# Kernel with four attention layers: reloads of the first layer's split weights issued at another place of ScalarE's program

## The chip, the cores and the metric

The kernel runs on one core of a Trainium2 chip. The metric is the device time of one execution in microseconds (us); lower is better. The core has TensorE (matmuls; PE in the profile, its weight loads PEld), VectorE (DVE), ScalarE (ACT), GpSimd (POOL) and SyncE (SP), and 16 DMA engines that serve the transfers issued by any of them.

## The reference, cut to what matters

Four layers follow each other. Only the first is touched. It is attention over 16 heads of 64 channels, for 8 batch elements of 512 positions, with two sets of weights, one for each half of the positions:

```python
for i in range(2):                                   # columns 0:256 and 256:512
    h = jnp.einsum('od,bdl->bol', Wq_list[i], z1ss[:, :, s:e])
    h = h + jnp.einsum('od,bdl->bol', Wi_list[i], u1ss[:, :, s:e])
q, k, v = jnp.split(w_heads, 3, axis=1)
rq = q + r_w_bias[None, :, :, None]
score = jnp.einsum('bndi,bndj->bnij', rq, k) * SCALE
prob = jax.nn.softmax(score, axis=-1)
attn_vec = jnp.einsum('bnij,bndj->bndi', prob, v)
attn_out = jnp.einsum('od,bdl->bol', Wo, attn_vec) + bo[None, :, None]
x = attn_out + z1ss                                  # then a layer norm
```

Here z1ss and u1ss have 8 x 256 x 512 elements and all is float32. The other three layers (a recurrent one, two attentions with an MLP, a non-local block) follow unchanged.

## The kernel before

`l0_attention` splits its work into 64 units (`HALF`). A unit is one batch element and one pair of heads; unit n has `bp, pair, l = where(n)`: turn `bp` (4 turns of two batch elements), `pair` of heads (8) and lane `l` (which of the turn's two elements). So two neighbouring units use the same weights, and each pair of heads comes back in every turn.

For precision each operand is held as a high and a low part, and a product is three matmuls. The weights of queries and keys for a pair are `w_hi[i]` and `w_lo[i]` with i = pair % 2: two buffers of 1 MB for each part. The value weights cover two pairs and lie in one buffer for each part, `wv_hi` and `wv_lo`. In the first turn (units 0 to 15) they are split on the chip and stored to DRAM (`w_scratch`, `wv_scratch`). In the three later turns they are only loaded back: `load_w`, L683 to L692, on ScalarE's DMA queue. With t = pair counted over all turns (8 to 31), there are 24 loads for each part of w, and 12 for each part of wv (even t alone). A load into w[i] must come after the last projection that used pair t-2, and ahead of the first that uses pair t.

Each engine runs a program written out by hand over n; semaphores alone tie them. TensorE in iteration n does: first half of the scores of unit n (L453), the projections of queries and keys for unit n+1 (L419, 48 matmuls), second half of the scores, the sums' transposes of n-1 (L462), the output projection of n-2 (L492), the weighing of values of n-1 (`weigh_values`, L478, 32 matmuls in two halves f = 0 and f = 1), and, if pair(n+1) is even, the value projection of unit n+1 (L437, 48 matmuls). So of four iterations two have a value projection: n = 3 and 0 (mod 4) do, 1 and 2 don't. Matmuls for w of pair t start in iteration 2t-1 (unit 2t).

ScalarE in iteration n: exponentials of the first half (L576), `queries(n+1)` (L599), `outputs(n-2)`, `keys(n+1)` (L583), `sums(n-1)`, exponentials of the second half, then `load_w`, then first-turn splits, `weighed(n-1)`, `values(n+1)`. `load_w` is called with part = 1-l: in iteration 2t-3 (l = 1) the high part of pair t, with `wv_hi` ahead of it if t is even, and in iteration 2t-2 (l = 0) the low part, with `wv_lo` ahead of it if t is even. Ahead of them stands a wait for the projections that used the buffer (`projected`).

The probabilities of a unit are turned in two halves: VectorE transposes 32x32 blocks in place (L778), then 16 DMAs of 64 KB for each half move the blocks from `prob` to `probT` (L281, `move`): 9 on SP's queue and 7 on POOL's. POOL does its part behind `scale_outputs` and `spread_sums`. Half f = 0 of unit n is moved in the middle of iteration n, half f = 1 at the start of iteration n+1; both are used by `weigh_values(n)` late in iteration n+1. A ring of three buffers (`RING`) makes ScalarE's exponentials wait for the half moved three halves before (`half_moved`).

SyncE also issues loads of x and u and of the accumulators, and their stores, at the start of a turn (`load_x`, `load_acc`, `store_acc`).

Of the kernel before, what the change touches and what calls it, by code (L numbers as in the profile page):

```python
# [6 lines left out]
F32 = mybir.dt.float32  # L7
# [11 lines left out]
LANES = 2  # L19
TURNS = B // LANES  # L20
# [134 lines left out]
def l0_attention(nc, kept, first, d, x, u, att, x1):  # L155

    D, HP = 64, 8
# [7 lines left out]
    QUADS = HP // 2  # L165
# [7 lines left out]
    def where(n):  # L173

        t, l = n // LANES, n % LANES
        return t // HP, t % HP, l
# [19 lines left out]
    def scratch(name, shape):  # L196
        return nc.dram_tensor(name, shape, F32, kind="Internal").ap()

    w_scratch = [scratch(f"kept_w_{part}", (HP, P, KT, 2, 2, P)) for part in ("hi", "lo")]
    wv_scratch = [scratch(f"kept_wv_{part}", (QUADS, P, KT, 2, 2, P)) for part in ("hi", "lo")]  # L200

    with Phase(nc, "l0") as ph:
# [4 lines left out]
        w_hi, w_lo = [[ph.sb(f"w_{part}{i}", [P, KT, 2, 2, P], F32R) for i in range(2)] for part in ("hi", "lo")]  # L207
        wv_hi, wv_lo = [ph.sb(f"wv_{part}", [P, KT, 2, 2, P], F32R) for part in ("hi", "lo")]
# [23 lines left out]
        w_stored, wv_stored = [ph.sem(f"w_stored{i}") for i in range(2)], ph.sem("wv_stored")  # L232
        w_in, wv_in = [ph.sem(f"w_in{i}") for i in range(2)], ph.sem("wv_in")
# [23 lines left out]
        def full(eng, s):  # L257

            eng.wait_ge(s.full, s.k + 1)
# [5 lines left out]
        def half_moved(eng, i):  # L265

            eng.wait_ge(moved_sp[i % RING], 16 * BY_SP * (i // RING + 1))
            eng.wait_ge(moved_pool[i % RING], 16 * (len(MOVES) - BY_SP) * (i // RING + 1))
# [15 lines left out]
        def projected(eng, n):  # L284

            full(eng, S[f"v{n}_1"] if where(n)[1] % 2 == 0 else S[f"k{n}"])

        with ph.block() as block:
# [278 lines left out]
            def _(act):  # L567
                def exponentials(n, its):
                    i = 2 * n + its[0] // 2
                    if i >= RING:  # L570
                        half_moved(act, i - RING)
                    for it in its:
                        for h in H2:
                            s = S[f"s{n}_{it}{h}"]
                            act.wait_ge(max_ready, 2 * IT * n + 2 * it + h + 1)
                            act.activation(prob[i % RING][:, :, it % 2, h, :].rearrange("p (q t) s -> p t q s", q=Q),  # L576
                                           s.ap[:, :].rearrange("p (t q s) -> p t q s", t=IT, q=Q), ACT.Exp, bias=nmax[:, n % 2, it, h:h + 1],
                                           accum_out=rsum[:, n % 2, it, h:h + 1]).then_inc(s.drained, 1)

                def keys(n):  # L580
                    s, l = S[f"k{n}"], where(n)[2]
                    full(act, s)
                    act.activation(k_hi[l][:, :], s.ap[:, :], ACT.Copy, scale=SCALE).then_inc(k_hi_ready, 1)  # L583
# [11 lines left out]
                def queries(n):  # L595
                    bp, pair, l = where(n)
                    s = S[f"q{n}"]
                    full(act, s)
                    act.activation(q_hi[l][:, :], s.ap[:, :], ACT.Identity, bias=rb[:, pair:pair + 1]).then_inc(q_hi_ready, 1)  # L599

                def sums(n):
                    s = S[f"r{n}"]
                    full(act, s)
                    act.wait_ge(scaled, n)
                    act.activation(rT[:, :], s.ap[:, :], ACT.Copy).then_inc(s.drained, 1)
# [8 lines left out]
                def outputs(n):  # L614
                    act.wait_ge(scaled, n + 1)
                    if n:
                        full(act, S[f"w{n - 1}_{RT - 1}"])
                    act.activation(oT_hi[:, :], oT[:, :], ACT.Copy).then_inc(oT_hi_ready, 1)
# [7 lines left out]
                def split_w(p):  # L626
                    act.wait_ge(wraw_in, 16 * p)
                    if p >= 2:
                        projected(act, LANES * (p - 2) + 1)
                        act.wait_ge(w_stored[p % 2], 32 * (p // 2))  # L630
                    act.activation(w_hi[p % 2][:, :, :, :, :], wraw[:, :, :, :, :], ACT.Copy).then_inc(w_hi_ready, 1)
# [8 lines left out]
                def split_wo():  # L640
                    act.wait_ge(wo_in, 16)
                    act.activation(wo_hi[:, :, :], wo_raw, ACT.Copy).then_inc(wo_hi_ready, 1)
# [39 lines left out]
                    for r in range(RT):  # L682
                        act.activation(xf[:, r, :], xf[:, r, :], ACT.Identity, bias=nb[:, r:r + 1], scale=sd[:, r:r + 1]).then_inc(xn_ready, 1)  # L683

                def load_w(t, part):
                    p, i = t % HP, t % 2
                    projected(act, LANES * (t - 2) + 1)
                    if i == 0:
                        act.wait_ge(wv_stored, 32 * QUADS)
                        act.dma_start((wv_hi, wv_lo)[part][:, :, :, :, :].bitcast(F32), wv_scratch[part][p // 2]).then_inc(wv_in, 16)  # L690
                    act.wait_ge(w_stored[i], 32 * QUADS)
                    act.dma_start((w_hi, w_lo)[part][i][:, :, :, :, :].bitcast(F32), w_scratch[part][p]).then_inc(w_in[i], 16)  # L692

                for h in H2:
                    own = slice(h * RT, (h + 1) * RT)
# [12 lines left out]
                for n in range(HALF):  # L708
                    bp, pair, l = where(n)
                    exponentials(n, (0, 1))  # L710
                    if n + 1 < HALF:
                        queries(n + 1)
                    if n > 1:
                        outputs(n - 2)
                    if n + 1 < HALF:
                        keys(n + 1)
                    if n:
                        sums(n - 1)
                    exponentials(n, (2, 3))
                    t = (n - 1) // LANES + 2  # L720
                    if HP <= t < TURNS * HP:
                        load_w(t, 1 - l)
                    if n == 0:
                        split_wo()
                    if bp == 0 and l == 0 and pair + 1 < HP:
                        split_w(pair + 1)
                    if bp == 0 and l == 1 and pair % 2 == 0 and pair + 2 < HP:
                        split_wv(pair // 2 + 1)
                    if pair == HP - 1 and bp + 1 < TURNS:
                        split_x(bp + 1, l)  # L730
                    if n == BIAS:
                        bias_rows()
                    if n == CENTRE:
                        centred()
                    if n:
                        weighed(n - 1)
                    if n + 1 < HALF:
                        values(n + 1)
                    if n == SUMMED:
                        moments()  # L740
                    if n == NORMED:
                        normed()
# [2488 lines left out]
```

## Time and profile before

| what | value |
|---|---|
| median of 3 runs | 3445.14 us (3443.86 to 3448.17) |
| the profiled execution's own time | 3442.56 us |
| its span, first to last instruction | 3440.5 us |
| granted TensorE clock, mean over the span | 0.949 |
| TensorE busy | 3115.6 us, 91% of the span |
| first layer | the first 1,300 us of the span, about 38% |

The durations below come from the one profiled execution. Its own time is 2.1 us over its span and 2.6 us under the median of the runs. A granted clock of 1.00 in a stretch is TensorE's full clock of 2.4 GHz, 0.5 is 1.2 GHz.

### The profile page before, as it was taken

The page shows a single profiled execution, that of the slowest core. Times are in us where ns is not written, and L with a number is a line of the kernel's source. Part 1 is how long each engine was busy: PE and PEld are TensorE (multiplying, and loading weights), DVE is VectorE, ACT ScalarE, POOL GpSimd, SP SyncE. Part 2 cuts the span into 40 slices and gives each one's busy share as a digit, 9 for nine tenths or more (in the row PEclk, how much of TensorE's full clock was granted, in tenths as well). Part 3 has the DMA queues.
Part 4 walks back from the last instruction along what each step waited for, and adds up shares of the span by engine and source line. Part 5 has one row for each costly group of instructions (what it writes and reads, how often), then busy time and mean ns, then how long its engine had stood idle before and what let it go on. Part 6 is the DMA issues. An engine that isn't in the chain of part 4 may idle for free. (4 is left out here: it accounts for less than half of the span.)

```text
span 3440.5 us, 55581 instructions
## 1 busy us (share of the span) xinstructions
PE 3115.6 (91%) x20384; PEld 2400.2 (70%) x20384; DVE 2362.2 (69%) x3589; ACT 1742.2 (51%) x4185; POOL 701.2 (20%) x1207
## 2 busy tenths in 40 slices
PE   7998999999998996799999997589999999699998
PEld 6777777777777774566666664378887787488885
DVE  6776666666675662999999999257777888543212
ACT  4454444544454543355566553247777777432222
POOL 2444444544444441000000000011101111000000
PEclk9999999999999998899999998789999999899999
DMA  7668766666675655445555444210011110310004
GB/s 245 209 218 268 225 184 183 207 212 197 197 234 162 207 143 187 121 96 123 116 117 120 104 109 104 59 64 14 26 56 56 44 44 29 108 50 12 25 13 167
DMA packets 179676, 434.78 MB, mean 126 GB/s; under 512 B 52912, under 2 KB 61104, under 8 KB 154960
## 3 DMA queue, kind: packets, MB, share of 16 engines
q1 hardware_dynamic: 120256, 262.17, 26.9%
q10 hardware_dynamic: 28304, 106.09, 8.6%
q0 software_dynamic: 30848, 62.97, 7.3%
q8 instruction: 164, 2.69, 0.3%
q14 instruction: 104, 0.85, 0.1%
HBM read 233.95 MB, written 62.91 MB: 86 GB/s over the span
## 5 line engine op out<-in xcount | busy, mean ns | idle before, releaser
L281 POOL DMA_DIRECT2D l_probT<-l_prob x896 | 441.2, 500 | 258.6 <-DVE l_prob L778 238.8
L756 DVE TENSOR_REDUCE l_nmax<-l_bank 128x1 f32<-128x512 f32 x512 | 317.0, 681 | 198.2 <-PE l_bank L453 198.2
L576 ACT ACTIVATE l_prob<-l_bank,l_nmax 128x512 f32<-128x512 f32 x512 | 344.5, 688 | 135.1 <-DVE l_nmax L756 120.5
L419 PE MATMUL l_bank<-l_x_hi,l_w_hi 128*128 128x256 f32 x1024 | 307.6, 300 | 75.4 <-DMA l_w_lo<-kept_w_lo 54.5
L778 DVE STREAM_TRANSPOSE l_prob<-l_prob 128x1024 f32<-128x1024 f32 x256 | 314.4, 1228 | 16.3 <-DVE l_acc L799 9.7
L419 PE MATMUL l_bank<-l_x_hi,l_w_lo 128*128 128x256 f32 x1024 | 299.8, 293 | 0.0
L419 PE MATMUL l_bank<-l_x_lo,l_w_hi 128*128 128x256 f32 x1024 | 299.0, 292 | 0.0
L1817 DVE TENSOR_TENSOR_SCAN l_kv<-l_wx,l_kv 128x2056 f32<-128x2056 f32 x64 | 283.8, 4435 | 3.1 <-DVE l_sxc L1938 1.5
L419 PEld LDWEIGHTS l_bank<-l_x_hi,l_w_hi 128*128 128x128 f32 x1024 | 207.0, 202 | 99.5 <-DMA l_w_lo<-kept_w_lo 59.2
L2391 ACT ACTIVATE l2a_sc<-l2a_sc,l2a_nmax 128x256 f32<-128x256 f32 x512 | 254.7, 508 | 41.1 <-DVE l2a_nmax L2507 41.1
L478 PE MATMUL l_bank<-l_probT,l_v 128*64 128x256 f32 x2048 | 248.6, 397 | 25.9 <-issue 12.5
L478 PEld LDWEIGHTS l_bank<-l_probT,l_v 128*64 128x64 f32 x2048 | 147.9, 142 | 121.6 <-issue 44.0
L2507 DVE CUSTOM_DVE_ANT_0 l2a_sc<-l2a_sc,l2a_mb 128x256 f32<-128x256 f32 x512 | 217.1, 484 | 0.0
L419 PEld LDWEIGHTS l_bank<-l_x_hi,l_w_lo 128*128 128x128 f32 x1024 | 207.1, 202 | 0.0
L419 PEld LDWEIGHTS l_bank<-l_x_lo,l_w_hi 128*128 128x128 f32 x1024 | 206.7, 202 | 0.0
L2500 DVE SCALAR_TENSOR_TENSOR l2a_sc<-l2a_bank,l2a_m 128x512 f32<-128x512 f32 x256 | 158.7, 681 | 54.1 <-PE l2a_bank L2263 54.1
L380 POOL TENSOR_TENSOR l_oT<-l_oT,l_rT 128x512 f32<-128x512 f32 x64 | 99.8, 1559 | 455.5 <-ACT l_oT L612 455.5
L2871 DVE TENSOR_TENSOR l2b_h_lo<-l2b_hf,l2b_h_hi 128x512 fp32r<-128x512 f32 x64 | 44.0, 691 | 199.3 <-ACT l2b_h_hi L2814 199.3
L2807 ACT ACTIVATE l2b_hf<-l2b_bank,l2b_b 128x512 f32<-128x512 f32 x64 | 44.0, 688 | 255.4 <-PE l2b_bank L2749 255.4
L1809 DVE TENSOR_TENSOR l_kv<-l_vb,l_ik 128x2048 f32<-128x2048 f32 x64 | 145.9, 2279 | 6.4 <-DMA l_vb<-vd 5.9
L437 PE MATMUL l_bank<-l_wv_hi,l_x_hi 128*128 128x256 f32 x512 | 148.1, 289 | 1.9 <-DVE l_wv_lo L815 1.9
L2274 PE MATMUL l2a_bank<-l2a_ident,l2a_sc 128*128 128x128 f32 x1024 | 133.2, 277 | 16.6 <-DVE l2a_oT L2520 8.7
(348 smaller groups left out, 7989.3 us busy)
## 6 DMA issues: line engine op xcount, KB each, us to landing
l_probT<-l_prob SPq DMA_DIRECT2D x1152, 64.0 KB, 2.7
l_vb<-vd SPq DMA_DIRECT2D x64, 1024.0 KB
l_probT<-l_prob POOLq DMA_DIRECT2D x896, 64.0 KB, 2.4
l_w_hi<-kept_w_hi ACTq DMA_DIRECT2D x24, 1024.0 KB, 7.2
l_w_lo<-kept_w_lo ACTq DMA_DIRECT2D x24, 1024.0 KB, 7.7
l_wv_hi<-kept_wv_hi ACTq DMA_DIRECT2D x12, 1024.0 KB, 5.4
l_wv_lo<-kept_wv_lo ACTq DMA_DIRECT2D x12, 1024.0 KB, 5.6
kept_w_hi<-l_w_hi SPq DMA_DIRECT2D x8, 1024.0 KB, 9.8
```

Source lines behind the costliest of these rows:

```text
L281: eng.dma_start(probT[i % RING][r * SQ:(r + 1) * SQ, g, :, :, :, :], prob[i % RING][g * SQ:(g + 1) * SQ, r * IT:(r + 1) * IT, :, :, :]).th ...
L419: mm = pe.matmul(s.ap[:, c * ROWS:(c + 1) * ROWS], a[:, kt, c, g, :], b[:, kt, c * ROWS:(c + 1) * ROWS], start=m == 0, stop=m == 3 * KT - 1)
L437: mm = pe.matmul(s.ap[:, at], a[:, kt, jt * P:(jt + 1) * P], b[:, kt, c, :, :], start=m == 0, stop=m == 3 * KT - 1)
L478: mm = pe.matmul(s.ap[own, f * ROWS:(f + 1) * ROWS], v[l][:, pair % 2, j, own], half[:, :, :, j, h, :], start=j == 0, stop=j == IT - 1)
L576: act.activation(prob[i % RING][:, :, it % 2, h, :].rearrange("p (q t) s -> p t q s", q=Q), s.ap[:, :].rearrange("p (t q s) -> p t q s", t ...
L756: dve.tensor_reduce(nmax[:, n % 2, it, h:h + 1], s.ap[:, :], AX.X, ALU.max, negate=True).then_inc(max_ready, 1)
L778: dve.transpose(own, own).then_inc(turned, 1)
L1809: dve.tensor_tensor(kv[n % NK][:, :, 1:ROWS + 1], vb[n % NV][:, :, :], ik[:, ct, :].unsqueeze(1).to_broadcast([P, NJ, ROWS]), ALU.mult).th ...
L1817: dve.tensor_tensor_scan(own, wx[:, :, :].rearrange("p j t -> p (j t)"), own, 0.0, ALU.mult, ALU.add)\
L2391: ins = act.activation(to[:, r, :], to[:, r, :], ACT.Exp, scale=-1.0, bias=nmax[:, k % SC_RING, i, r:r + 1], accum_out=rsum[:, k % SC_RING ...
L2500: dve.scalar_tensor_tensor(out=sc[k % SC_RING][i][:, :, :], in0=s.ap[:, :].rearrange("p (r j) -> p r j", r=RT), scalar=HD ** -0.5, in1=own ...
L2507: dve.tensor_tensor_reduce(out=to[:, r, :], in0=to[:, r, :], in1=own[:, r, :], scale=-1.0, scalar=3.0e38, op0=ALU.add, op1=ALU.min, accum_ ...
```

## The change

In turns 1 to 3 the loads are issued elsewhere in ScalarE's program. Both parts of w for pair t go out in one iteration, 2t-3, right behind the first half's exponentials and ahead of `queries(n+1)`. The two parts of wv go out in the next iteration, 2t-2, at the same place, for even t. The number of loads, their sizes, their queue and the semaphores they count on are unchanged.

```diff
-                def load_w(t, part):
+                def load_w(t):
                     p, i = t % HP, t % 2
                     projected(act, LANES * (t - 2) + 1)
-                    if i == 0:
-                        act.wait_ge(wv_stored, 32 * QUADS)
-                        act.dma_start((wv_hi, wv_lo)[part][:, :, :, :, :].bitcast(F32), wv_scratch[part][p // 2]).then_inc(wv_in, 16)
                     act.wait_ge(w_stored[i], 32 * QUADS)
-                    act.dma_start((w_hi, w_lo)[part][i][:, :, :, :, :].bitcast(F32), w_scratch[part][p]).then_inc(w_in[i], 16)
+                    for part, to in enumerate((w_hi, w_lo)):
+                        act.dma_start(to[i][:, :, :, :, :].bitcast(F32), w_scratch[part][p]).then_inc(w_in[i], 16)
+
+                def load_wv(g):
+                    projected(act, LANES * 2 * (g - 1) + 1)
+                    act.wait_ge(wv_stored, 32 * QUADS)
+                    for part, to in enumerate((wv_hi, wv_lo)):
+                        act.dma_start(to[:, :, :, :, :].bitcast(F32), wv_scratch[part][g % QUADS]).then_inc(wv_in, 16)
...
                     exponentials(n, (0, 1))
+                    t = (n - 1) // LANES + 2
+                    if HP <= t < TURNS * HP:
+                        if l == 1:
+                            load_w(t)
+                        elif t % 2 == 0:
+                            load_wv(t // 2)
                     if n + 1 < HALF:
                         queries(n + 1)
...
                     exponentials(n, (2, 3))
-                    t = (n - 1) // LANES + 2
-                    if HP <= t < TURNS * HP:
-                        load_w(t, 1 - l)
```

## Rows read from the trace of the kernel before

**Rows 1.** The page: busy time of each engine.
```profile
PE 3115.6 (91%) x20384; PEld 2400.2 (70%) x20384; DVE 2362.2 (69%) x3589; ACT 1742.2 (51%) x4185; POOL 701.2 (20%) x1207
```

**Rows 2.** Waits of PE, 311 to 1290 us: total, times, longest.
```profile
PE l_bank L419 <- DMA l_w_lo<-kept_w_lo: 54.5, 11, 6.8
...
PE l_bank L478 <- DMA l_probT<-l_prob: 1.2, 1, 1.2
```

**Rows 3.** Busy time by stretch: iterations 20 to 23, one each.
```profile
core 0: us, PE busy (x) PEld busy (x) DVE busy (x) ACT busy (x) POOL busy (x), PEclk, DMA share, GB/s
433.93:454.59 20.66, 20.66 (x163) 17.38 (x162) 12.93 (x18) 9.65 (x23) 8.67 (x17) 1.00 0.51 155
454.59:469.30 14.71, 14.71 (x115) 11.56 (x114) 12.44 (x18) 8.46 (x21) 3.53 (x8) 1.00 0.46 137
469.30:484.02 14.72, 14.72 (x116) 11.64 (x114) 12.93 (x19) 8.46 (x21) 8.67 (x16) 1.00 0.93 278
484.02:512.39 28.37, 22.74 (x164) 19.46 (x162) 13.52 (x19) 9.66 (x23) 13.80 (x25) 0.88 0.67 190
```

**Rows 4.** Timeline of PE, end of iteration 22 and start of 23.
```profile
480.42 3.67 PE L478 MATMUL l_bank<-l_probT,l_v 128*64 128x256 f32 x32
484.02 0.50 PE L453 MATMUL l_bank<-l_k_hi,l_q_hi 64*128 64x512 f32 x2
...
491.33 0.58 PE L419 MATMUL l_bank<-l_x_hi,l_w_hi 128*128 128x256 f32 x1 [5.63 <-DMA l_w_lo<-kept_w_lo]
```

**Rows 5.** Timeline of ACT in iteration 22: exponentials, q_hi, the last issue.
```profile
471.10 0.69 ACT L576 ACTIVATE l_prob<-l_bank,l_nmax 128x512 f32<-128x512 f32 x1 [1.08 <-DVE l_nmax L756]
...
474.08 0.69 ACT L599 ACTIVATE l_q_hi<-l_bank,l_rb 128x512 fp32r<-128x512 f32 x1 [0.20 <-PE l_bank L419]
...
479.62 0.68 ACT L576 ACTIVATE l_prob<-l_bank,l_nmax 128x512 f32<-128x512 f32 x1
...
481.13 0.45 ACTq L692 DMA_DIRECT2D l_w_lo<-kept_w_lo  x1
```

**Rows 6.** The low part of w issued at 481.1: issue to landing.
```profile
DMA to landing us min/median/max: 10.2/10.2/10.2
```

**Rows 7.** All 48 loads of w (L692): issue to landing.
```profile
DMA to landing us min/median/max: 4.8/7.3/11.4
```

**Rows 8.** Busy time by stretch: iterations 15, 19, ..., 47 and 59 (ten).
```profile
327.08:355.13 28.05, 22.92 (x166) 19.59 (x164) 18.59 (x23) 11.39 (x24) 13.21 (x20) 0.88 0.65 197
...
1199.19:1228.79 29.60, 23.04 (x164) 19.75 (x163) 13.53 (x19) 9.65 (x23) 13.80 (x25) 0.88 0.64 183
sum 281.01, PE 227.18 PEld 194.24 DVE 152.79 ACT 102.08 POOL 138.86; mean PE 22.72 PEld 19.42 DVE 15.28 ACT 10.21 POOL 13.89
```

**Rows 9.** Moves on SP's queue, 469.6 to 475.8 us (durations, first and last start).
```profile
L281 SPq DMA_DIRECT2D l_probT<-l_prob x9: 507/597/912, 469.8 to 475.7; - x9
...
DMA to landing us min/median/max: 3.7/3.9/6.1
```

**Rows 10.** Moves on POOL's queue in the same stretch, from its timeline.
```profile
471.88 3.47 POOL L281 DMA_DIRECT2D l_probT<-l_prob  x7
```

**Rows 11.** Moves on SP's queue, 448.9 to 454.6 us.
```profile
L281 SPq DMA_DIRECT2D l_probT<-l_prob x9: 507/592/894, 449.1 to 454.5; - x9
...
DMA to landing us min/median/max: 2.0/2.8/3.1
```

**Rows 12.** DMA queues, 468 to 472 us: packets, MB, share; issues below.
```profile
q10 hardware_dynamic: 212, 1.61, 95.9%
...
l_probT<-l_prob SPq DMA_DIRECT2D x4, 64.0 KB, 4.1
```

**Rows 13.** DMA queues, 476 to 480 us (q0 is POOL's, q1 SP's).
```profile
q0 software_dynamic: 261, 0.55, 59.3%
q1 hardware_dynamic: 272, 0.37, 38.9%
```

**Rows 14.** Timeline of PE in iteration 14, second half of weigh_values.
```profile
325.20 0.44 PE L478 MATMUL l_bank<-l_probT,l_v 128*64 128x256 f32 x2 [1.18 <-DMA l_probT<-l_prob]
```

## The prediction

> **What bounds the kernel now.** I read four views in this order. The page first: TensorE is busy 91% of the span, every other engine less [rows 1]. An average over four layers proves little, so next the busy time by stretch, cut at the starts of four iterations of the first layer, in the steady state of turn 1 [rows 3]. The reader is to see that in iterations 20, 21 and 22 TensorE is busy for the whole stretch at a granted clock of 1.00 (2.4 GHz): 20.66 us with a value projection, 14.7 without. VectorE, the next one, has 12.9 of 14.7 us. Iteration 23 does the same work as iteration 20 and takes 28.37 us, at a clock of 0.88. Third, the waits of TensorE alone: one line holds 54.5 us in 11 waits, on the load of the low part of w [rows 2]. Fourth, the timeline there: the first half's scores start at 484.02, and the first projection starts at 491.33 after 5.63 us of nothing [rows 4]. That load was issued at 481.13 and took 10.2 us: 481.1 + 10.2 = 491.3, the very start of the matmul [rows 5, 6]. So in this place the end is set by when ScalarE issues a load, and everywhere around it by TensorE.
>
> The waits come at even t alone. There the low part of w is issued right behind `wv_lo`, and in an iteration without a value projection, so it has 14.7 us less what ScalarE has used up: from 481.13 to the wish of TensorE at 485.7 is 4.6 us, for a load that takes 4.8 to 11.4 [rows 4, 5, 7].
>
> **What the removed waits are worth.** Ten iterations (n = 15, 19, 23, ..., 47 and 59) have this wait. Together they last 281.01 us [rows 8]. Without it each would last what iteration 20 lasts, so 281.01 - 10 x 20.66 = 74.4 us. That is more than the waits themselves (54.5 with the eleventh, of 0.7 in iteration 51, whose stretch is long for other reasons; 53.8 for the ten). The rest, 20.6 us or 2.1 each, is TensorE at its lower level of 1.2 GHz: the clock fell during the wait and rose again some matmuls after it, and the stretch has 22.74 us of busy TensorE where iteration 20 has 20.66 [rows 3]. It goes with the waits: the undisturbed stretches around show 1.00.
>
> **The change part by part.** *Loads of w.* Pair t's two parts are now issued in iteration 2t-3, behind the first half's exponentials. In iteration 22 these start at 471.10, 1.8 us into the iteration; the issue stood 1.5 us behind the first exponential of its half (479.62 to 481.13), so now it comes about 3.0 to 3.3 us into an iteration [rows 3, 5]. TensorE wants w 1.7 us into iteration 2t-1 [rows 4]. For even t that is two iterations of 14.7 less 1.5: 28 us; for odd t two of 20.66: 40 us. The slowest of all loads took 11.4 us [rows 7]. The wait is gone with over 15 us to spare.
>
> *Loads of wv.* They are issued 3 us into iteration 2t-2 and wanted at the end of iteration 2t-1, behind `weigh_values`: 11.7 + 14.7 = 26 us. Also early enough.
>
> *ScalarE's program.* The number of issues is the same, 72. Two now stand ahead of `queries(n+1)`; they take 0.33 to 0.45 us each of the sequencer, some 0.8 together [rows 5]. Four exponentials of 0.69 us are then still to run, to 473.9, and q_hi can't start before 474.08, when TensorE has the product [rows 5]. So I cost this at nothing. If that cover were gone it would be 0.8 x 36 = 29 us on ScalarE, which is busy 8.5 of 14.7 us, so still not on the path. The wait `projected` ahead of the loads asks for the projection of unit 2t-3, which TensorE did in iteration 2t-4, ahead of any score of iteration 2t-3: it holds back neither the loads nor `queries`, `keys` and the second exponentials that are queued behind it. The stores it also waits for are those of the first turn; the last were issued one to three iterations earlier.
>
> *What is late next: the moves of the probabilities.* This is the unknown term. The loads share the 16 DMA engines with 64 moves of 64 KB in two iterations. In iteration 22 SP issues the nine moves of the second half of unit 21 from 469.8 to 475.7 and the last lands 6.1 us later, at 481.8; POOL issues its seven from 471.88 [rows 9, 10]. `weigh_values` starts at 480.42 and needs that half after half of its 3.67 us, at 482.25 [rows 4]. So 0.4 us are left today, with two loads issued 3.4 to 3.8 us ahead of the moves. The quiet case is at 449.1: last issue 454.5, landed 3.1 later, 8.5 us in all [rows 11]. Put at 469.8 it would end at 478.3, 3.9 us ahead of the need.
>
> After the change the two loads go out at about 472.3, 2.5 us behind the first move, not 3.4 ahead. From 468 to 472 the loads' queue had 95.9% of all 16 engines and moved 1.61 MB, 0.42 MB a us, while four moves already issued stood still [rows 12]; two loads of 1.05 MB so hold the engines for 5.0 us. Lower bound of the lateness: 0, if the moves get turns between (a gain is excluded, since TensorE has nothing else to win there). Middle: all 5.0 us fall on the moves, 478.3 + 5.0 = 483.3, 1.05 us late. Upper: a load takes 10.2 us [rows 6], landing at 482.8, and the half of the moves left over then drains at the rate that moves alone reach, 0.92 MB in 4 us, so 0.5 MB in 2.2 [rows 13]: 485.0, 2.8 us late.
>
> How often: moves of a second half stand in this window in iterations that follow one without a value projection, n = 2 and 3 (mod 4). In the other two they are issued before the iteration begins (449.1 against 454.59) and are done when the loads go out. Loads fall there for wv (12 times, n = 2) and for odd t of w (12 times, n = 3): 24 places. I take 0.5 us each, between nothing and 1.05, because before a load starts about 40% of the moves are through and a queue with little left needs few turns: 24 x 0.5 = 12 us. Ends: 0 and 24 x 2.8 = 67. A wait of this kind exists already, 1.2 us once [rows 2, 14], and shows what it looks like.
>
> **Sum.** Against the profiled execution's own time: 3442.6 - 74.4 - 0.7 + 12 = 3379.5. The median of the runs is 2.6 above that execution: 3382 us.
>
> **The rivals.** (1) *The moves aren't hurt at all.* The loads only rearrange 16 engines' work that fits: a share of 0.93 in iteration 22, 0.46 in iteration 21 [rows 3]. Then 3370 us. For it: the queues take turns of some sort, since moves did land by 481.8. Against it: the loads held 95.9% of the engines while moves waited [rows 12]. The Trainium skill, "DMA: Bandwidth & Descriptors", section "Queues, rings and completion order", has it that each engine takes turns among the queues, a packet of typically 9 to 17 descriptors at a time. By that rule the moves would lose little, and the result would be this rival's 3370; the trace agrees only in part [rows 11, 12], since the moves issued there landed 4.1 us after issue, against 2.8 in the quiet case.
>
> (2) *The moves starve*: 2 to 2.8 us late at 24 places, 48 to 67 us, gives back most of the gain: 3418 to 3437, say 3425. For it: 0.4 us are left now, and the DMA share is 0.93 already. Against: before, the loads delayed them too, from 8.5 to 12.0 us, and TensorE didn't wait.
>
> (3) *The other side: TensorE waits at `weigh_values` for over 3.1 us at 24 places.* From there 24 x 3.1 = 75 us eat the gain. With waits of 4 us the clock falls too (2.1 each): 24 x 6.1 = 146, so 3370 + 146 = 3516. It needs moves landing 16 us after the first issue where they have taken 12.0.
>
> (4) *The change does nothing*, since something else ends the wait at the same moment (x split, VectorE): 3445. Against: iteration 20 does all that iteration 23 does, in 20.66 us.
>
> **How the numbers follow.** My forecast (some lateness, 3374 to 3400) gets 0.52, rival 1 0.19, rival 2 0.18, rival 3 0.04, rival 4 0.03; 0.04 lies between them. The range goes from 3366 (rival 1 less the scatter of the runs) to 3416, which leaves out most of rival 2 and rivals 3 and 4. What a measurement of this kernel can tell from no change is 0.2%, 6.9 us: faster means below 3438. Faster 0.91, same 0.05, slower 0.04.
>
> **What would show it.** In the profile after: no wait of L419 on a load of w, iterations 15, 19, 23 and so on at 20.7 us and clock 1.00; a mean clock above 0.949; a line "PE L478 <- DMA l_probT" in the waits, with some 12 us in up to 24 waits. If that line has 40 or more, rival 2 holds; if it is still near 1.2, rival 1. The prediction is wrong if iterations n = 2 and 3 (mod 4) grow by 3 us or more, or if the long iterations stay at 26 to 30 us.

## The result, and the profile after

The changed kernel takes 3486.66 us (median of 4 runs, 3486.11 to 3489.57), the kernel before 3444.5 (4 runs, 3443.21 to 3448.17). The ratio is 1.0122 with a 95% interval of 1.0105 to 1.014: 42 us slower, where I had forecast 63 us faster. The profiled execution took 3489.57 us.

The page of the changed kernel, its span and the busy time of each engine:

```profile
span 3487.6 us, 55569 instructions
...
PE 3125.5 (90%) x20384; PEld 2394.4 (69%) x20384; DVE 2361.4 (68%) x3589; ACT 1743.5 (50%) x4185; POOL 699.7 (20%) x1207
```

Every engine has the same work as before [rows 1]. What changed is who waits. The waits of TensorE from 311 to 1338 us, to be read against [rows 2]:

```profile
PE l_bank L478 <- DMA l_probT<-l_prob: 61.9, 19, 8.0
PE l_bank L478 <- issue: 19.8, 2, 10.6
PE l_bank L492 <- ACT first_anx L659: 7.8, 1, 7.8
```

The wait of L419 on a load of w is gone, all 54.5 us of it. In its place stands a wait of L478, `weigh_values`, on the moves of the probabilities, which had 1.2 us. The busy time by stretch of the changed kernel, iterations 20 to 24, against [rows 3]:

```profile
core 0: us, PE busy (x) PEld busy (x) DVE busy (x) ACT busy (x) POOL busy (x), PEclk, DMA share, GB/s
447.38:468.04 20.66, 20.66 (x164) 17.37 (x163) 12.93 (x18) 9.67 (x23) 8.66 (x17) 1.00 0.36 98
468.04:482.75 14.71, 14.71 (x115) 11.55 (x115) 12.44 (x18) 8.47 (x21) 3.52 (x8) 1.00 0.76 242
482.75:504.78 22.03, 16.68 (x117) 12.21 (x116) 13.40 (x19) 8.47 (x21) 8.67 (x16) 0.85 0.72 193
504.78:527.76 22.98, 20.99 (x164) 17.41 (x162) 12.92 (x18) 9.67 (x23) 13.81 (x25) 0.99 0.77 214
527.76:548.42 20.66, 20.66 (x163) 17.37 (x162) 13.02 (x18) 9.56 (x23) 8.69 (x17) 1.00 0.37 105
```

Iteration 23 fell from 28.37 to 22.98 us, but iteration 22, which took 14.72, takes 22.03: the pair went from 43.09 to 45.01. The timeline of TensorE in the changed kernel, in iteration 22, and then the one wait in iteration 23, shows where:

```profile
493.87 1.95 PE L478 MATMUL l_bank<-l_probT,l_v 128*64 128x256 f32 x16
...
501.16 0.69 PE L478 MATMUL l_bank<-l_probT,l_v 128*64 128x256 f32 x2 [5.35 <-DMA l_probT<-l_prob]
...
519.95 0.44 PE L478 MATMUL l_bank<-l_probT,l_v 128*64 128x256 f32 x2 [1.99 <-DMA l_probT<-l_prob]
```

The first half of `weigh_values` runs on time; the second is ready at 495.81 (501.16 less 5.35) and its probabilities are not there until 501.1. The wait of 5.35 us and 1.97 us of lower clock (16.68 busy us, where the quiet iteration has 14.71) are the 7.31 us by which the iteration grew. TensorE's granted clock went from 2.4 to 1.2 GHz at 498.26, within the wait, and back at 505.09, just inside iteration 23.

The sum by iteration, 0 to 62, comes to 45.7 us, of 47.1 by which the span grew:

| iterations | before | after | difference |
|---|---|---|---|
| the ten long ones (15, 19, ..., 47, 59) | 281.0 | 260.5 | -20.5 |
| n = 2 (mod 4), from 14 to 58 | | | +52.5 |
| 0, 4, 16, 48, 51, 55 | | | +13.8 |
| n = 0 and 1 (mod 4) in the steady state | 20.66, 14.71 | 20.66, 14.71 | 0 |

The ten would last 206.6 us without any wait. So of the 74.4 us to be had, 53.9 were given back in the very same iterations, 25.8 of them in iterations 19 and 35 (33.19 and 33.91 us), at the starts of turns. In the third row, iterations 16 and 48 (2.4 and 3.5 us longer) have waits of L419, and the inputs are late there: SP's loads of x and u for the next turn landed 4.6 to 6.9 us after their issue before, 12.0 to 15.2 after, and ScalarE, which has to split them, now waits (311 to 1338 us):

```profile
ACT l_x_hi L624 <- DMA l_xraw<-in_u: 22.6, 3, 8.2
```

Now from the late half back to its cause. ScalarE's queue in the changed kernel, iteration 22: the last two loads, and `q_hi` behind them:

```profile
486.31 0.33 ACTq L696 DMA_DIRECT2D l_wv_hi<-kept_wv_hi  x1
...
486.67 0.46 ACTq L696 DMA_DIRECT2D l_wv_lo<-kept_wv_lo  x1
...
487.52 0.69 ACT L599 ACTIVATE l_q_hi<-l_bank,l_rb 128x512 fp32r<-128x512 f32 x1 [0.19 <-PE l_bank L419]
```

Then SP's moves of the wanted half (483.2 to 488.9 us), with the time from issue to landing, to be read against [rows 9, 11]:

```profile
L281 SPq DMA_DIRECT2D l_probT<-l_prob x9: 507/594/997, 483.3 to 488.8; - x9
...
DMA to landing us min/median/max: 1.9/4.9/12.3
```

The moves were issued on time: nine in 5.5 us (5.9 before). The last landed 12.3 us after its issue, at 501.1; the quiet case has 3.1 [rows 11], the case with loads ahead 6.1 [rows 9]. The issues are not late; the transfers are slow. The DMA queues of the changed kernel from 489 to 496 us (packets, MB, share of 16 engines; q10 holds the loads, q0 POOL's moves, q1 SP's):

```profile
DMA packets 510, 2.25 MB, mean 321 GB/s; under 512 B 124, under 2 KB 124, under 8 KB 299
...
q10 hardware_dynamic: 227, 1.73, 78.1%
q0 software_dynamic: 144, 0.32, 15.1%
q1 hardware_dynamic: 139, 0.20, 9.9%
```

In 7 us the moves' two queues got 0.52 MB, the wanted half and the unit's own first half together. In the 5 us after it, as the loads ended, they got 1.06 MB:

```profile
q1 hardware_dynamic: 442, 0.60, 55.1%
q0 software_dynamic: 234, 0.46, 40.8%
q10 hardware_dynamic: 25, 0.07, 6.2%
```

From here on I use one measure: L, from the first issue of a half's 16 moves to the last landing, for the half that `weigh_values` needs. The medians are over units 21 to 46: those whose half is used in iterations n = 2 (mod 4), seven of them, and those used in n = 3, six of them without unit 34 at the start of a turn. TensorE needs the half 12.55 us after the first issue in n = 2 (483.26 to 495.81 in iteration 22) and some 13 after it in n = 3. Before, L had a median of 9.9 us in n = 2 and 10.4 in n = 3; after, 16.2 and 15.7.

### The profile page after: what moved, and what is told of

It is laid out like the page before. It is cut to its first block and busy times, and to the rows that moved or that the text cites. A ratio compares the mean times of both kernels' runs of the same rounds, so it can differ in the third digit from the quotient of the medians.

```text
span 3487.6 us, 55569 instructions
## 1 busy us (share of the span) xinstructions
PE 3125.5 (90%) x20384; PEld 2394.4 (69%) x20384; DVE 2361.4 (68%) x3589; ACT 1743.5 (50%) x4185; POOL 699.7 (20%) x1207
## 3 DMA queue, kind: packets, MB, share of 16 engines
q1 hardware_dynamic: 120256, 262.17, 26.8%
## 5 line engine op out<-in xcount | busy, mean ns | idle before, releaser
L478 PE MATMUL l_bank<-l_probT,l_v 128*64 128x256 f32 x2048 | 266.6, 414 | 109.4 <-DMA l_probT<-l_prob 66.6
L419 PE MATMUL l_bank<-l_x_hi,l_w_hi 128*128 128x256 f32 x1024 | 298.1, 291 | 24.9 <-DVE l_x_lo L854 11.3
L478 PEld LDWEIGHTS l_bank<-l_probT,l_v 128*64 128x64 f32 x2048 | 152.0, 147 | 214.3 <-DMA l_probT<-l_prob 76.1
L419 PE MATMUL l_bank<-l_x_hi,l_w_lo 128*128 128x256 f32 x1024 | 291.3, 284 | 0.0
L419 PE MATMUL l_bank<-l_x_lo,l_w_hi 128*128 128x256 f32 x1024 | 291.1, 284 | 0.0
L419 PEld LDWEIGHTS l_bank<-l_x_hi,l_w_hi 128*128 128x128 f32 x1024 | 197.7, 193 | 48.6 <-issue 39.4
L419 PEld LDWEIGHTS l_bank<-l_x_hi,l_w_lo 128*128 128x128 f32 x1024 | 198.0, 193 | 0.0
L419 PEld LDWEIGHTS l_bank<-l_x_lo,l_w_hi 128*128 128x128 f32 x1024 | 197.9, 193 | 0.0
```

Source lines behind the costliest of these rows:

```text
L419: mm = pe.matmul(s.ap[:, c * ROWS:(c + 1) * ROWS], a[:, kt, c, g, :], b[:, kt, c * ROWS:(c + 1) * ROWS], start=m == 0, stop=m == 3 * KT - 1)
L478: mm = pe.matmul(s.ap[own, f * ROWS:(f + 1) * ROWS], v[l][:, pair % 2, j, own], half[:, :, :, j, h, :], start=j == 0, stop=j == IT - 1)
```

## The experiments

**Place or grouping (four runs).** Theory A: what costs is the place of the issue, about 3 us behind the first of the moves; the new grouping by itself is good. Rival: the grouping costs, 2 MB at once. The first run keeps the grouping and goes back to the old place:

```diff
                     exponentials(n, (0, 1))
-                    t = (n - 1) // LANES + 2
-                    ...
-                            load_wv(t // 2)
...
                     exponentials(n, (2, 3))
+                    t = (n - 1) // LANES + 2
+                    ...
+                            load_wv(t // 2)
```

> The new grouping (both parts of w in iteration 2t-3, both of wv in 2t-2), but issued at the old place, behind the second half's exponentials. Theory A (the loss comes from the place: loads that go out 3 us behind the first move stand amid the moves of the half that weigh_values needs next): 3370 to 3385 us, the waits of L478 on moves near 0 to 10 us, the moves of iteration 22 landed about 10 to 12 us after the first issue. Rival B (4 MB of moves and loads in one short iteration are too much for the DMA engines, wherever in it the loads go out; the grouping does it): 3440 to 3490 us, waits of L478 on moves over 40 us.

Measured: 3382.45 us (3373.22 to 3395.5), ratio 0.9815 (0.9778 to 0.9851), mean clock 0.956. The busy time by stretch of this run, iterations 22 and 23:

```profile
455.95:470.66 14.71, 14.71 (x116) 11.56 (x114) 12.92 (x19) 8.47 (x21) 8.70 (x16) 1.00 0.88 275
470.66:491.32 20.66, 20.66 (x164) 17.37 (x162) 13.42 (x19) 9.67 (x23) 13.85 (x25) 1.00 1.02 303
```

Both iterations are at their floor, the second with the DMA engines full throughout. L is 10.3 and 11.0 us, under 12.55. A gain of the forecast size is in the grouping, at the old place. The ten long iterations sum to 218.5 us; only those at a turn's start (19, 31, 35, 47) are over 21, at 22.3 to 25.1. That the time equals my forecast of 3382 for the changed kernel is chance: the 12 us that stay over the floor of 206.6 lie at the starts of turns, and not in 24 small waits.

The second run is the other half of the change, the old grouping in the new place (`load_w(t, 1 - l)` with the old body, behind `exponentials(n, (0, 1))`).

> The old grouping (high parts in iteration 2t-3, low parts in 2t-2, wv with them for even t), issued at the new place, behind the first half's exponentials. Theory A (place): iterations n = 2 (mod 4) still carry 2 MB amid the moves and grow by 3 to 5 us, n = 3 carry 1 MB and grow by 1 to 2, so 3435 to 3465 us, with moves on L478 over 40 us. Rival B (grouping): about 3370 us.

Measured: 3465.94, ratio 1.0061 (1.0041 to 1.0082), just above what was expected. Waits of TensorE in this run:

```profile
PE l_bank L478 <- DMA l_probT<-l_prob: 54.6, 17, 8.3
```

The wait is there without the new grouping. Away from the starts of turns, iterations n = 2, which still get 2 MB for even t, take 18.6 to 22.1 us (L 16.4); n = 3 with 1 MB at a time take 20.7 to 21.7, for a floor of 20.66 (L 12.8). So the place makes the wait and the bytes at the place size it.

The third leaves the later loads of the value weights out (`load_wv` gone, and TensorE's wait for them replaced by one for the splits of the first turn).

> The changed kernel with the 24 reloads of wv left out (so the value projections of turns 1 to 3 use the value weights of the last pair). Theory A: iterations n = 2 (mod 4) go back to 14.7 us (about 52 us of excess in the changed kernel), those with n = 3 keep some 2 to 5 us each; 3400 to 3425 us. Rival C (the issues ahead of queries hold up ScalarE): all iterations but n = 2 unchanged and n = 2 shorter by under 1 us, 3475 us or more.

Measured: 3450.36, ratio 1.0009 (0.9995 to 1.0023): a miss by 25 us and more. Iterations n = 2 are back at 14.7, as expected (L 8.2), but n = 3 take 23.8 to 32.6, with L unchanged at 15.7 us. The miss is in iterations 15, 31 and 47, which went up by 8.6, 3.9 and 9.5 us, to 30.28, 30.63 and 31.22. There the wanted half's first move is issued 4.9 us into the iteration, where in the changed kernel it is issued 0.2 us in, because the iteration ahead stands for its own wait meanwhile. Two neighbouring stalls had shared one lateness; taking one away does not save it. This is why a count of places times a price does not add here.

The fourth keeps the new place, but only in iterations that follow one with a value projection, whose moves are through by then:

```diff
-                        if l == 1:
+                        if l == 1 and t % 2 == 0:
                             load_w(t)
-                        elif t % 2 == 0:
                             load_wv(t // 2)
+                        if l == 0 and t % 2:
+                            load_w(t)
```

> The new place, but only in iterations that follow one with a value projection: w and wv of even t together (4 MB) in iteration 2t-3, w of odd t in 2t-2; none in iterations n = 2 and 3 (mod 4). Theory A (only loads amid the moves that are wanted next hurt): 3368 to 3385 us, waits of L478 on moves under 10 us. Rival B (too much traffic in short iterations): 4 MB in iteration n = 1 should wait there or in n = 2, 3430 us or more. Rival C (issues ahead of queries): as the changed kernel, 3486 us.

Measured: 3435.79, ratio 0.9972 (0.9955 to 0.999), short of the expected gain. In the steady state n = 3 is at its floor of 20.65, with L at 7.9 us. But 4 MB now go out in the iteration before n = 2, are not done when its moves start (L 14.1), and n = 2 takes 16.3 to 20.4. The last of the four loads issued in iteration 21 landed 18.2 us after its issue; at 0.42 MB a us [rows 12] 4.2 MB need 10 us of all engines. So a backlog hurts too, not only a load behind the moves.

**The place, swept (three runs).** With the new grouping, the block of loads put ahead of `exponentials(n, (0, 1))`, behind `queries(n + 1)`, and behind `sums(n - 1)`:

> The new grouping, issued one step earlier in the same iteration: ahead of the first half's exponentials, so about with the first move (0 to 0.5 us into the iteration). Theory A, in its simple form (loads hold all 16 engines for their 5 us, and the moves issued by then and later wait for that): the moves land 8 + 4 = 12 to 13 us after the first issue, 0 to 1 us late, 3375 to 3400 us. Rival D (any load in flight together with the moves costs the same, ahead or behind): about 3486 us, as the changed kernel.

> The new grouping, issued one step later: behind queries(n+1), about 5 us into the iteration, when most moves of the wanted half have been issued and some 60% have landed. Theory A: the tail of them is still hit, though less; 3400 to 3450 us. Rival D: about 3486 us.

> The new grouping, issued behind sums(n-1), just ahead of the second half's exponentials, about 10 us into the iteration: the wanted half's moves have landed in the quiet case (8.5 us after the first issue). Theory A: 3370 to 3385 us, like the old place. Rival C (issues ahead of exponentials hold up ScalarE): above 3400 us.

| place in ScalarE's iteration | median us | ratio (95%) | waits of L478 on moves: us, times |
|---|---|---|---|
| ahead of exponentials 0, 1 | 3449.68 | 1.0028 (1.0014 to 1.0043) | 41.6, 17 |
| behind them (the changed kernel) | 3486.66 | 1.0122 (1.0105 to 1.014) | 61.9, 19 |
| behind `queries` | 3475.72 | 1.0098 (1.0083 to 1.0113) | 48.9, 15 |
| behind `sums` | 3426.56 | 0.9954 (0.994 to 0.9967) | 10.9, 3 |
| behind exponentials 2, 3 (first run) | 3382.45 | 0.9815 (0.9778 to 0.9851) | 1.9, 2 |

The changed kernel has the slowest of five places, though its interval overlaps that of the place behind `queries`. In n = 2, L is 13.7 us with the loads issued 0.3 us ahead of the first move (0.18 and 0.50 us into iteration 22), 16.2 with them 3.1 us behind it, 15.8 with 4.3, 9.7 with 9.4 (most moves are through), and 10.3 with the loads of the last iteration, 3.4 to 3.8 us ahead. I had expected 3375 to 3400 of the first place; 0.3 us ahead of the moves is not enough. The fourth place (behind `sums`) is at the floor in the steady state, 14.72 and 20.67 us for iterations 22 and 23, so the rival of issues that hold up ScalarE, which had expected the time above 3400, has no support there. The place loses around the starts of turns (iterations 16, 19, 35 and 48 take 29.86, 35.11, 32.24 and 27.45), which my sum over the steady state left out. In 16 and 48 it is the inputs again: ScalarE waited 21.8 us in three for the load of u.

**Smaller pieces.** If a queue of smaller loads let the moves in between, four DMAs of 256 KB for each load would help:

```diff
-                        act.dma_start(to[i][:, :, :, :, :].bitcast(F32), w_scratch[part][p]).then_inc(w_in[i], 16)
+                        for kt in range(KT):
+                            act.dma_start(to[i][:, kt, :, :, :].bitcast(F32), w_scratch[part][p][:, kt, :, :, :]).then_inc(w_in[i], 16)
```

> The changed kernel with each load of 1 MB cut into four DMAs of 256 KB (one for each kt, rows of 2 KB in place of 8 KB), same place, same bytes. Theory E (a load's share on an engine passes as one piece, so small pieces let the moves in between): waits of L478 on moves fall by half or more, 3400 to 3445 us. Rival F (bytes on the engines count, not pieces; smaller rows are no faster): 3480 to 3510 us.

Measured: 3507.76, ratio 1.0189 (1.017 to 1.0208). L did fall, to 13.4 and 13.8 us, and TensorE has no wait of L478 on moves left. But the issues back up on ScalarE. Its timeline in this run, then its waits and TensorE's longest one from 311 to 1338 us:

```profile
499.64 3.85 ACTq L698 DMA_DIRECT2D l_wv_lo<-kept_wv_lo  x4
503.54 0.69 ACT L599 ACTIVATE l_q_hi<-l_bank,l_rb 128x512 fp32r<-128x512 f32 x1 [5.39 <-issue]
```

```profile
ACT l_q_hi L599 <- issue: 162.0, 35, 6.7
...
PE l_bank L492 <- DVE l_oT_lo L796: 75.9, 30, 5.2
```

`q_hi` is held back 35 times, at 36 places, and `outputs`, which stands behind it in ScalarE's program, makes TensorE's output projection (L492) wait. My cost of nothing for issues ahead of `queries` rested on 0.33 to 0.45 us each, which held in iteration 22 of the changed kernel (`q_hi` waited 0.19 us above). Of its 72 issues 16 took over 0.5 us; of the 288 here 174 did, with 2.4 us for the longest in iteration 23, and the cover was gone. Since `weigh_values` itself now comes later, this run doesn't tell how much of the wait the smaller pieces by themselves would save.

**The starts of turns (three runs with one edit).** SP's program at the start of a turn, in the changed kernel (timeline, iterations 18 and 19):

```profile
395.39 5.83 SPq L281 DMA_DIRECT2D l_probT<-l_prob  x9
401.32 0.53 SPq L295 DMA_DIRECT2D l_xraw<-in_x  x1
401.89 0.56 SPq L296 DMA_DIRECT2D l_xraw<-in_u  x1
402.50 0.54 SPq L305 DMA_DIRECT2D att<-l_acc  x1
416.80 0.37 SPq L301 DMA_DIRECT2D l_acc<-in_x  x1
417.26 18.61 SPq L281 DMA_DIRECT2D l_probT<-l_prob  x27
```

SP stands for 13.7 us between the store of an accumulator (L305) and the load into the same one (L301), and every move behind it stands too. Its waits, first of the changed kernel:

```profile
SPq L301 <- DMA att<-l_acc: 47.2, 6, 13.7
```

and of the kernel before, where the same store lands 7.5 us after its issue and not 14.3:

```profile
SPq L301 <- DMA att<-l_acc: 27.1, 6, 7.3
```

Late moves of unit 18 then cost TensorE 9.2 us, and 10.6 at the start of a later turn (its two waits on "issue"). To take SP out of the wait for the store, `load_acc` moves from behind `store_acc` to the middle of SP's next iteration:

```diff
+                    if bp and (pair, l) in ((0, 1), (1, 0)):
+                        load_acc(bp, 1 - l)
...
-                        load_acc(bp, l)
```

> The changed kernel with load_acc moved from behind store_acc to the middle of SP's next iteration, so that SP does not wait for the store to land with the next nine moves queued behind that wait. Theory G (a second loss: at turn starts the store lands late behind the loads, SP stands up to 13.7 us, and TensorE waits 9 to 10 us in iterations 19 and 35): 3455 to 3470 us, those two iterations under 28 us. Rival A alone (all of the loss is loads against moves, the wait of SP costs nothing): within 5 us of 3487.

> The old place with the new grouping (3382 us), and load_acc moved in the same way. Theory G: iterations 19 and 35, 24.5 and 25.1 us there, go to 20.7 to 22: 3372 to 3379 us. Otherwise 3380 to 3385 us.

> Loads behind sums(n-1) (3427 us) and load_acc moved. Its steady iterations were already at 14.7 and 20.7 us; the loss lay at turn starts. Theory G: iterations 19 and 35 (35.1 and 32.2 us) come down by 8 us or more each: 3395 to 3412 us. The waits for x in iterations 16 and 48 stay. If the wait of SP is not the cause: 3420 us or more.

Measured: on the changed kernel 3477.16 (1.0102, 1.0071 to 1.0134), short of the 17 us or more that were expected and not clear of the changed kernel's interval, with iterations 19 and 35 at 32.19 and 31.15 us and not under 28; on the first run's version 3396.9 (0.9865, 0.9833 to 0.9896), no gain; on the version behind `sums` 3429.7 (0.9955, 0.9939 to 0.997), nothing. The timeline of SP in the second says why:

```profile
392.86 1.73 SPq L305 DMA_DIRECT2D att<-l_acc  x1
394.68 6.71 SPq L281 DMA_DIRECT2D l_probT<-l_prob  x9
408.05 0.37 SPq L301 DMA_DIRECT2D l_acc<-in_x  x1
```

The store took 15.2 us to land, at 408.0, and SP now stood for it between the two halves of unit 18 instead. The edit moved the wait and didn't remove it. So the wait was tested again with a third accumulator, taken from `anx`, so that no load waits for the store just made:

```diff
-        acc = [ph.sb(f"acc{l}", [P, RT, COLS]) for l in range(LANES)]
+        acc = [ph.sb(f"acc{j}", [P, RT, COLS]) for j in range(2)] + [first["anx"][:, 1, :, :]]
...
-                    if bp:
-                        sp.wait_ge(acc_stored[l], 16 * bp)
+                    if bp * LANES + l >= 3:
+                        sp.wait_ge(acc_stored[1 - l], 16 * (bp - 1 + l))
```

> The changed kernel with the third accumulator buffer. Theory G: SP stands nowhere, iterations 19 and 35 from 33 us to under 27, 3462 to 3472 us; the rest of the loss stays. If the wait costs nothing: 3484 to 3490 us.

> Old place, new grouping (3382 us), and a third accumulator buffer (the half of anx that is free until iteration 51), so that load_acc at a turn's start waits for no store that has just been issued. Theory G (SP's wait for the store holds up the nine moves behind it): SP waits on att<-l_acc near 0, iterations 19 and 35 from 24.5 and 25.1 us to about 21, 3370 to 3378 us. If bytes at the turn's start matter and not the wait: 3380 us or more.

On the changed kernel 3468.4, ratio 1.0078 (1.0057 to 1.0099): 15 us (by the ratios) to 18 us (by the medians) of its loss were this wait. Iteration 19 went from 33.19 to 26.5 us, as expected, iteration 35 from 33.91 to 30.4 only. On the first run's version 3391.45, ratio 0.9842 (0.9827 to 0.9857), against 3388.16 for that version without it, beside it on the same chip: nothing. The wait of L301 is gone from SP's list there, yet iterations 19 and 35 take 26.8 and 30.4 us (25.7 and 28.0 without the third buffer). So there it isn't SP's standing that costs. That it is the bytes in flight (moves, loads, x, u and accumulators together) is what is left, and is not shown.

**Whose bytes (two runs).** Rival I: the late half suffers from the loads. Theory H: it suffers as much from the other moves, those of the unit's own first half. These are held back by one more transpose in n = 2 and 3:

```diff
-            eng.wait_ge(turned, IT * n + 2 * f + 2)
+            held = f == 0 and n % 4 in (2, 3) and n >= 14
+            eng.wait_ge(turned, IT * n + 2 * f + 2 + held)
```

> The changed kernel, but in iterations n = 2 and 3 (mod 4) from 14 on the moves of the unit's own first half wait for one more transpose, so that they no longer go out 6 us behind the wanted half's moves and the loads. Theory H (the wanted half is 8 us late and not 5 because the next half's moves share the engines with it and with the loads): the wanted half lands 12 to 14 us after its first issue in place of 15 to 18, waits of L478 on moves fall by half, 3420 to 3465 us. Rival I (loads and moves alone slow each other): landing stays at 15 to 18 us, 3480 us or more.

Measured: 3483.01, ratio 1.0113 (1.0081 to 1.0144); L478 waits 59.0 us in 22. The edit did what it should: the own first half of unit 22 went out 14.0 us into the iteration and not 6.2. L fell by 1.1 and 1.7 us, to 15.1 and 14.0. So it is the loads for the most part. Its queues from 484 to 495 us:

```profile
DMA packets 729, 2.81 MB, mean 256 GB/s; under 512 B 213, under 2 KB 213, under 8 KB 477
...
q10 hardware_dynamic: 283, 2.06, 58.8%
```

Near the end of this stretch most engines are done, and the order of what is left can be seen. From 493.2 to 494.2 us, in steps of 25 ns:

```profile
GB/s 0 0 328 0 0 0 0 0 0 0 0 0 0 0 0 82 0 0 328 0 0 0 0 0 0 0 0 0 0 0 82 0 0 0 328 0 0 0 0 0
...
q10 hardware_dynamic: 3, 0.02, 5.9%
q1 hardware_dynamic: 3, 0.00, 1.1%
```

A packet of the loads (8 KB: 328 GB/s over 25 ns) and one of SP's moves (2 KB: 82 GB/s) start in turn; the third packet of q1 has next to no bytes. The three of q10 fill 5.9% of 16 us of engine time, 0.31 us each.

And the bytes halved: the low parts are not loaded again in turns 1 to 3, so each place has 1 MB.

> The changed kernel with the reloads of the low parts left out, of w and of wv (turns 1 to 3 compute with the low parts of the last pairs): 1 MB at each of the 36 places in place of 2. Price linear in bytes: half the loss at the 24 places, some 1.8 us each, 3415 to 3440 us. Price with a threshold (the moves have 3.9 us in hand, and 1 MB takes 2.5 us): under 0.7 us each, 3370 to 3392 us.

Measured: 3421.81, ratio 0.9929 (0.991 to 0.9947); waits of L478:

```profile
PE l_bank L478 <- DMA l_probT<-l_prob: 22.4, 14, 4.5
```

In n = 2, L is 12.7 us: 8.2 with no load (the run that leaves the value weights out), 12.7 with 1 MB, 16.2 with 2 MB. The first MB costs 4.5 us, the second 3.5; L grows from the first MB on. Since 12.55 us are there, 1 MB is about 0.2 us late at the median and 2 MB 3.7. The time lies in the range of the linear price.

**The better version again**, the same kernel as in the first run:

> The same kernel as the first experiment (old place, new grouping), on the chip of these runs, so that the third buffer is compared beside it: 3375 to 3390 us, ratio 0.978 to 0.985.

Measured: 3388.16 (3384.14 to 3392.77), ratio 0.9836 (0.9822 to 0.9851). It beats both kernels: 1.6% under the one before, 98 us under the changed one.

## Why the prediction was wrong

*What bounds the kernel, and what the removed waits are worth:* right. The wait of L419 is gone, and the new grouping at the old place brought 60 us, with six of the ten long iterations at 20.66 to 20.92. *ScalarE's program at nothing:* right for the change as made (`q_hi` waited 0.19 us).

*The step that failed* is the size of the term "What is late next": "I take 0.5 us each, between nothing and 1.05 [...]: 24 x 0.5 = 12 us", with 2.8 as its end. The mechanism, the place (second half of `weigh_values`) and the iterations (n = 2 and 3) were right. The size was 5.35 us in iteration 22, and 7.3 with the clock. Over the layer, what was given back is 53.9 + 52.5 + 13.8 = 120 us, where the term had 12; 15 to 18 of the 120 are SP's wait for the store. I had even my own warning row: loads 3.4 us ahead of the moves had pushed L from 8.5 to 12.0.

Three assumptions around the term were off, each in the same direction:

- *The moves would be 40% through and the rest needs few turns.* In the 7 us from 489 to 496 they got 0.52 MB, half of one half. What counts is the bytes that a load puts in front: about 4.5 us for the first MB and 3.5 for the second (the run with the high parts alone), where my middle had 5.0 for both.
- *A load amid moves takes at most 10.2 us.* `wv_lo`, issued at 486.67, took 14.7:

```profile
DMA to landing us min/median/max: 14.7/14.7/14.7
```

  The 0.42 MB a us of [rows 12] holds for loads alone. Mixed with the moves it was 0.32 (2.25 MB in 7 us above, all engines taken). With the first half held it was 0.26 (2.81 MB in 11 us), but there the queues filled only 82% of the engines, so 0.31 for the time in use.
- *The clock.* I priced it (2.1 us a wait) only in rival 3. The wait of 5.35 us brought 2.3 us of it: 1.97 in iteration 22 and 0.33 in iteration 23 (20.99 busy us for 20.66), where the stretch at 1.2 GHz ends. Not every wait brings it: the clock stayed at 2.4 GHz around the waits of 1.99 us in iteration 23, 3.52 in 38 and 2.82 in 42.

The Trainium skill, "DMA: Bandwidth & Descriptors", section "Queues, rings and completion order", says that an engine takes turns among queues by whole packets. The trace agrees in kind: packets of the two queues start in turn in the stretch at 493.2 us above. What the trace counts as a packet is a piece of at most 8 KB there; whether it is the packet of the page isn't shown. What I got wrong in rival 1 is what follows from turns. From 489 to 496 us a packet of the loads held an engine for 0.385 us (78.1% of 16 x 7 us, over 227), where it had 0.29 with the loads alone [rows 12], one of q0 for 0.12 and one of q1 for 0.08; a turn each is then most of the time for the load. Two loads are some 276 packets (2.1 MB at 7.6 KB), 17 for each engine, 6.6 us by this estimate; with the 1.1 us that the own first half costs it makes 7.7, where L grew by 8.0. That turns by packet are the whole cause is only argued. The counts aren't equal (227 for q10, 144 and 139 for the moves' queues), and in the run with rows of 2 KB q10 still had 576 packets against 158 and 208 from 499 to 506 us.

*What was missed.* The wait of SP for its own store at the starts of turns. I had priced what the loads do to the moves, and not what they do to the other transfers that are in flight at the same time. In the kernel before, SP stood 27.1 us in 6 waits for its stores, and the new place brought the longest from 7.3 to 13.7. It was worth 15 to 18 us of the changed kernel's loss, shown by the third accumulator. The loads of x and u are another such transfer: ScalarE's 22.6 us of waiting for u are new. What they cost was not measured apart.

*Rivals.* Rival 3 is what happened, by its mechanism: landings of over 16 us and waits of over 3.1 (61.9 us in 19, 3.3 each), clock and all. Its 3516 assumed 6.1 us at all of 24 places; 120 us over 24 are 5.0, the starts of turns included. My sign for rival 2, 40 us or more in the line of L478, was met as well (61.9); it is the time that tells the two apart. I gave rival 3 a chance of 0.04, since "landings have taken 12.0", and had argued against it with a row in which the loads had a head start. The run that leaves the value weights out also shows why a product of places and price misleads: a lateness at one place is paid once and gives the next place time.

What stays open: why loads issued level with the first move (the block ahead of the exponentials) make L longer in n = 3 than in n = 2, 15.2 against 13.7; and in the better version, what an ordering of bytes at turn starts would bring (iterations 19 and 35 are still 4 to 7 us over the floor). A version with the loads behind `weighed` or spread over both iterations in steps of 1 MB was not tried.

## What to carry to other kernels

When a bulk load moves in time, price it by the small transfers that it now lands on: find when they are issued, how long they have until they are wanted, and take for their delay the load's whole bytes at the mixed rate (2.1 MB at 0.32 MB a us here, 6.6 us), not a share of it. A load may be issued earlier by regrouping (what an iteration carries) or by moving within the iteration; test the two apart, as here one was worth 60 us and the other cost 98. And a queue whose engine waits for its own store passes any delay of that store on to all transfers behind it.

## What the runs showed of the hardware that was not expected

- Loads of 1 MB from DRAM and moves of 64 KB inside the chip together ran at 0.31 to 0.32 MB a us of engine time, the loads alone at 0.42; 2 MB issued 3 us behind the first move pushed the 16 moves' landing from 8.2 to 16.2 us, 1 MB to 12.7.
- The same store of an accumulator, 512 KB, landed 7.5 us after its issue before and 14.3 with the loads at the new place; loads of x and u landed in 4.6 to 6.9 us before and in 12.0 to 15.2 after.
- An issue on ScalarE's queue took over 0.5 us in 16 of 72 cases with two in a row (longest 1.9 us), and in 174 of 288 with eight (longest 2.4).
- With most engines done (493.2 to 494.2 us of the run with the first half held), packets of 8 KB from the loads' queue and of 2 KB from SP's followed each other in turn, one of each.
- Which side of the moves the loads stand on mattered more here than how full the engines were: the better version has a DMA share of 0.88 and 1.02 in iterations 22 and 23 and no wait; the changed kernel has 0.72 and 0.77 and waits in both.
